# A two-layer graph kernel on one core: four more blocks transposed by DMA, eight more loaded ahead, and the x1 stores moved behind the rounds of layer 0

## What is computed

```python
h = jnp.maximum(_layernorm(x), 0.0)
# layer 0: 4-bit activations, 3-bit weights
support = jnp.matmul(act_quant(h) / act_delta, weight_q / wgt_delta) * act_delta * wgt_delta
support_q = act_quant(relu(support))
x = x + jnp.matmul(adj / s, support_q / support_delta) * s * support_delta
# layer 1, with a symmetric, normalised matrix
h = jnp.maximum(_layernorm(x), 0.0)
S = (adj + adj.T) * 0.5 + I
S = dinv[:, None] * S * dinv[None, :]      # dinv = rowsum(S) ** -0.5
x = x + (adj @ S) @ h                      # taken as adj @ (S @ h)
```

## Time and profile before

| what | value |
|---|---|
| median of 3 runs | 505.09 us (504.79 to 523.74) |
| profiled execution | 509.47 us |
| its span | 507.7 us |
| TensorE busy | 489.5 us (96%) |
| VectorE busy | 275.9 us (54%) |
| ACT busy | 142.7 us (28%) |
| GpSimd busy | 36.5 us (7%) |
| granted clock, mean | 0.997 |

### The profile page before, as it was taken

The page is one execution under the profiler, slowest core; times in us unless marked ns, Lnnn a source line. Parts: engine busy times, 40 slices in busy tenths (PEclk is TensorE's granted clock), DMA queues, the critical chain, the costliest instruction groups (busy, mean ns, idle before and its releaser), DMA issues.

```text
span 507.7 us, 6439 instructions
## 1 busy us (share of the span) xinstructions
PE 489.5 (96%) x2446; PEld 242.4 (48%) x2446; DVE 275.9 (54%) x368; ACT 142.7 (28%) x199; POOL 36.5 (7%) x51
## 2 busy tenths in 40 slices
PE   1899999997999999999999999999999999999997
PEld 1756555553564444444444444444444444444446
DVE  4964779896979878787798767450001000100000
ACT  1885852434544153444432121240000000000000
POOL 1325511132000000000000000000000000000000
PEclk9999999998999999999999999999999999999999
DMA  8970577999934043323224332018001000010001
GB/s 293 402 298 1 187 167 207 196 168 211 305 117 146 0 125 105 102 94 113 83 83 126 104 103 83 0 48 304 21 22 41 21 21 21 21 41 21 21 21 43
DMA packets 39948, 56.89 MB, mean 112 GB/s; under 512 B 22904, under 2 KB 23160, under 8 KB 39928
## 3 DMA queue, kind: packets, MB, share of 16 engines
q1 hardware_dynamic: 37040, 46.15, 30.6%
q10 hardware_dynamic: 2888, 10.49, 7.4%
HBM read 42.99 MB, written 8.39 MB: 101 GB/s over the span
## 4 chain that ended last, share of the span: by engine, by line
PE 84%; DVE 7%; DMA 4%; ACT 2%; issue 1%; SPq 1%; POOL 0%; ACTq 0%
PE ps_a L1098 31%; PE ps_p L997 14%; PE ps_p L1061 7%; PE ps_a L1061 7%; PE ps_b L1061 7%; PE ps_m L1061 4%; PE ps_h L1061 4%; DMA feat<-in_x 2%; DMA at<-at 2%; PE ps_b L979 1%; PE ps_b L951 1%; PE ps_m L997 1%; PE ps_h L997 1%; PE ps_a L979 1%; DVE at L801 1%; DVE small L849 1%
## 5 line engine op out<-in xcount | busy, mean ns | idle before, releaser
L997 PE MATMUL ps_p<-small,at 128*128 128x512 f16 x448 | 102.6, 384 | 2.8 <-DMA at<-at 2.8
L920 DVE SCALAR_TENSOR_TENSOR feat<-ps_a,feat 128x512 f32<-128x512 f32 (+1 forms) x16 | 10.8, 675 | 148.7 <-PE ps_a L1098 144.2
L1098 PE MATMUL ps_a<-small,at 128*128 128x512 f16 x360 | 80.1, 379 | 0.0
L1098 PE MATMUL ps_a<-a_in,at 128*128 128x512 f16 x360 | 80.1, 379 | 0.0
L997 PEld LDWEIGHTS ps_p<-small,at 128*128 128x128 f16 x448 | 44.1, 99 | 52.2 <-issue 5.6
L499 ACT ACTIVATE split<-a_in 128x1024 f16<-128x1024 f32 x30 | 31.7, 1057 | 101.8 <-PE ps_p L1061 90.0
L1098 PEld LDWEIGHTS ps_a<-a_in,at 128*128 (+1 forms) x360 | 35.2, 98 | 42.5
L1098 PEld LDWEIGHTS ps_a<-small,at 128*128 (+1 forms) x360 | 35.2, 98 | 42.5
L845 DVE TENSOR_TENSOR split<-a_in,split 128x1024 f16<-128x1024 f32 x30 | 36.7, 1225 | 34.0 <-ACT split L499 34.0
L1061 PE MATMUL ps_p<-feat,split 128*128 (+1 forms) x180 | 43.9, 379 | 0.5 <-DVE small L849 0.5
L1061 PE MATMUL ps_a<-feat,split 128*128 (+1 forms) x180 | 43.7, 379 | 0.0
(11 more groups left out here) (178 smaller groups left out, 445.0 us busy)
## 6 DMA issues: line engine op xcount, KB each, us to landing
a_in<-in_adj SPq DMA_DIRECT2D x34, 512.0 KB, 3.7
a_in<-in_adj ACTq DMA_DIRECT2D x20, 512.0 KB, 5.0
out<-feat SPq DMA_DIRECT2D x31, 256.0 KB, 2.5
feat<-in_x SPq DMA_DIRECT2D x8, 512.0 KB, 11.3
at<-in_adj SPq DMA_DIRECT2D x8, 512.0 KB, 14.1
feat<-out SPq DMA_DIRECT2D x4, 1024.0 KB, 9.6
at<-in_L_gnn_weight SPq DMA_DIRECT2D x2, 512.0 KB, 3.8
split<-in_adj SPq DMA_DIRECT2D x1, 512.0 KB, 15.8
```

What stands on the lines that cost most here:

```text
L920: nc.vector.scalar_tensor_tensor(out, products, 1.0 / (SA * SZ), out, ALU.mult, ALU.add).then_inc(y_out, 1)
L997: last = nc.tensor.matmul(l0_bank(r), at_block(r, lo, j), small[:, j * D:(j + 1) * D], start=(j == 0 and lo == 0), stop=(j == T - 1 and lo ...
L1098: last = nc.tensor.matmul(BANK[n], at_block(t, lo, j), z_part(j, z_lo), start=(j == 0 and lo + z_lo == 0), stop=(j == T - 1 and lo == 1))
```

## The change

- Moved are units 3, 5, ..., 29 (fourteen) instead of 7, 9, ..., 25 (ten). `ADDED` has fifteen units instead of twelve. TensorE makes four turns fewer (3, 5, 27, 29); `acc` is still turned.
- Twenty units are loaded ahead instead of twelve: units 12 to 19 go to the scratch in tiles 10 to 13, as soon as `hT`, `sq`, `xq` and the weights there are done with. A unit `u` from 12 to 27 is written to a tile in which `waited_in(u)` stood, and its writers wait for these.
- Units 3 and 5 are split and moved ahead of round 1, 7 and 9 in round 1, and `2r + 7` in round `r` from 2 to 11: one round earlier than before, measured from their use.
- SP's queue now issues all loads (`rows_again` is its own), in the order of the diff. ACT's queue issues none.
- `store_x1(0)` to `store_x1(12)` are issued one behind the other, after `sums(5)`, instead of one a round.
- GpSimd's first copy into `acc` waits for `hT_ready` instead of `sq_ready`.

The diff, cut to its core:

```diff
-AHEAD = 12
+AHEAD = 20
-MOVED = tuple(range(7, 26, 2))
-ADDED = (1, 3) + MOVED
+MOVED = tuple(range(3, 30, 2))
+ADDED = (1,) + MOVED
...
+        def in_tile(u):
+            return u // 2 + 4
+        def waited_in(u):
+            return 2 * (u // 2) - 8, 2 * (u // 2) - 7
...
-        TURNS = {r: [2 * r + 4] for r in range(2, 11)}
-        TURNS.update({1: [4, 5, 6], 11: [26, 27], 12: [28, 29, "acc"], 13: [30, 31]})
-        ROW_SUMS = {4: [0, 1], 5: [2, 3], 6: [4, 5], 8: [6, 8], "acc": []}
-        MOVES = {r: [2 * r + 5] for r in range(1, 11)}
+        TURNS = {r: [2 * r + 4] for r in range(2, 12)}
+        TURNS.update({1: [4, 6], 12: [28, "acc"], 13: [30, 31]})
+        ROW_SUMS = {2: [0, 1], 4: [2, 4], "acc": []}
+        MOVES = {r: [2 * r + 7] for r in range(2, 12)}
+        MOVES[1] = [7, 9]
...
             sums(0)
             sums(1)
+            sp.wait_ge(hT_ps, T // 2)
+            rows(16)
+            rows(17)
+            move(3)
+            sp.wait_ge(sup_ps, T // 2)
+            for u in (18, 19, 12, 13):
+                rows(u)
+            sp.wait_ge(sq_ready, T // 2)
+            rows(14)
+            rows(15)
+            move(5)
+            for u in range(AHEAD, AHEAD + 4):
+                rows_again(u)
             for r in range(1, 12):
-                for u in MOVES.get(r, []):
+                if r >= 8:
+                    rows_again(2 * r + 9)
+                for u in MOVES[r]:
                     move(u)
-                store_x1(r - 1)
+                if r >= 8:
+                    rows_again(2 * r + 8)
             for v in range(2, 6):
-                free_slot(sp, UNITS - 6 + v)
+                free_slot(UNITS - 6 + v)
                 sums(v)
-            store_x1(11)
-            store_x1(12)
+            for t in range(13):
+                store_x1(t)
...
             scale_support(5)
+            hi_rows(3)
             scale_support(6)
             scale_support(7)
             hi_turned(2)
-            hi_turned(3)
+            hi_rows(5)
+            for w in ROW_SUMS[2]:
+                row_sum(w)
...
             clamp_rows(7)
+            lo_rows(3)
             clamp_support(6)
             clamp_support(7)
             lo_turned(2)
-            lo_turned(3)
+            lo_rows(5)
...
             layer0(0, [14, 15])
-            turn(3)
             for r in range(1, 14):
```

More of the change, by code:

```diff
@@ L97, in stage @@
         def stage(u, lo):
+            if u == 29:
+                return late(15, 2048 + lo * W, W, f16)
             return late(14, 2048 * (MOVED.index(u) % 2) + lo * W, W, f16)
@@ L116, in turn_no @@
             if u == "acc":
-                return turn_no(29) + 1
-            return TURNED.index(u) + (u > 29)
+                return turn_no(28) + 1
+            return TURNED.index(u) + (u > 28)
         def turn_bank(u):
@@ L202, in gnn_kernel @@
         at4 = at[:, :].rearrange("p (r two i) -> p r two i", two=2, i=N)
+        def in_tile(u):
+            return u // 2 + 4
+        def waited_in(u):
+            return 2 * (u // 2) - 8, 2 * (u // 2) - 7
         def unit_in(u):
             if RING <= u < AHEAD:
-                return late((9, 8, 7, 6)[(u - RING) // 2], u % 2 * 2 * W, W, f32)
+                return late(in_tile(u), u % 2 * 2 * W, W, f32)
             return a_in[:, (u % RING) * W:(u % RING + 1) * W]
@@ L270, in wait_moved @@
                 engine.wait_ge(at_moved[k % 2][lo], 16 * (k // 2 + 1))
[L272 to L284, removed]
         def arrivals(u):
@@ L293, in load_x, with rows, rows_again, free_slot @@
                 sp.dma_start(feat3[:, 2 * n:2 * n + 2, :], x_tiles[:, 2 * n:2 * n + 2, :]).then_inc(x_in[n], 16)
+            def rows(u):
+                sp.dma_start(unit_in(u), adj[(u // 2) * P:(u // 2 + 1) * P, (u % 2) * W:(u % 2 + 1) * W])\
+                  .then_inc(arr_sem(u), 16)
+            def rows_again(u):
+                free_slot(before(u))
+                rows(u)
+            def free_slot(u):
+                if u in ADDED:
+                    sp.wait_ge(acc_done, ADDED.index(u) + 1)
+                if u in MOVED:
+                    sp.wait_ge(lo_ready, MOVED.index(u) + 1)
+                else:
+                    sp.wait_ge(turned, turn_no(u) + 1)
+                    sp.wait_ge(rs_done, TURNED.index(u) + 1)
             def move(u):
@@ L297, in move @@
                     sp.wait_ge(ready, MOVED.index(u) + 1)
-                    if u == 13:
-                        free_slot(sp, 10 + lo)
+                    if u == 29:
+                        wait_moved(sp, 25)
+                        wait_moved(sp, 27)
+                    elif u >= 12:
+                        free_slot(waited_in(u)[lo])
                     sp.dma_start_transpose(at_half(u // 2, lo, u % 2).rearrange("p (b i) -> p b i", i=P), stage(u, lo))\
@@ L315, in _ @@
                 load_x(n)
-            rows(sp, 0)
-            rows(sp, 1)
+            rows(0)
+            rows(1)
             for n in range(2, T // 2):
                 load_x(n)
-            for u in range(2, AHEAD):
-                rows(sp, u)
+            for u in range(2, 12):
+                rows(u)
             sums(0)
             sums(1)
+            sp.wait_ge(hT_ps, T // 2)
[4 more added lines that the diff above has]
+            for u in (18, 19, 12, 13):
+                rows(u)
+            sp.wait_ge(sq_ready, T // 2)
[4 more added lines that the diff above has]
+                rows_again(u)
             for r in range(1, 12):
-                for u in MOVES.get(r, []):
+                if r >= 8:
+                    rows_again(2 * r + 9)
+                for u in MOVES[r]:
                     move(u)
-                store_x1(r - 1)
+                if r >= 8:
+                    rows_again(2 * r + 8)
             for v in range(2, 6):
-                free_slot(sp, UNITS - 6 + v)
+                free_slot(UNITS - 6 + v)
                 sums(v)
-            store_x1(11)
-            store_x1(12)
+            for t in range(13):
+                store_x1(t)
             for v in range(6, UNITS):
@@ L400, in _ @@
                 if k == 0:
-                    pool.wait_ge(sq_ready, T // 2)
+                    pool.wait_ge(hT_ready, T // 2)
                     nc.gpsimd.tensor_scalar(acc, unit_in(u), 0.0, 1.0, ALU.add, ALU.mult).then_inc(acc_done, 1)
@@ L428, in row_sum @@
                 nc.scalar.activation(unit_in(u), unit_in(u), ACT.Copy, accum_out=rowsum[:, u:u + 1]).then_inc(rs_done, 1)
-            def rows_again(u):
-                free_slot(act, before(u))
-                rows(act, u)
             def hi_rows(u):
@@ L445, in hi_turned @@
                 act.wait_ge(turned, turn_no(u) + 1)
-                if u == 12:
-                    act.wait_ge(rs_done, TURNED.index(10) + 1)
+                if 12 <= u < 28:
+                    act.wait_ge(rs_done, TURNED.index(waited_in(u)[0]) + 1)
                 nc.scalar.activation(at_half(u // 2, 0, u % 2), turn_bank(u)[:, :], ACT.Copy, scale=SA)\
@@ L533, in _ @@
                     if u == 28:
-                        wait_moved(act, MOVED[-2])
-                        wait_moved(act, MOVED[-1])
+                        wait_moved(act, 25)
+                        wait_moved(act, 27)
+                    elif u == 30:
+                        wait_moved(act, 29)
                     if u != "acc":
                         hi_turned(u)
[L538 to L541, removed]
                     if u == TURNS[r][0]:
@@ L546, in _ @@
                         row_sum(w)
-                        if w < 4 or 12 <= w < UNITS - 4:
-                            rows_again(w + (AHEAD if w < 4 else RING))
                 if r == 9:
@@ L661, in lo_turned, with lo_rows @@
                 dve.wait_ge(athi, TURNED.index(u) + 1)
-                if u == 12:
-                    dve.wait_ge(acc_done, ADDED.index(11) + 1)
-                    dve.wait_ge(lo_ready, MOVED.index(11) + 1)
+                if 12 <= u < 28:
+                    dve.wait_ge(acc_done, ADDED.index(waited_in(u)[1]) + 1)
+                    dve.wait_ge(lo_ready, MOVED.index(waited_in(u)[1]) + 1)
                 nc.vector.scalar_tensor_tensor(at_half(u // 2, 1, u % 2), turn_bank(u)[:, :], SA,
                                                at_half(u // 2, 0, u % 2), ALU.mult, ALU.subtract).then_inc(atlo, 1)
+            def lo_rows(u):
+                dve.wait_ge(hi_ready, MOVED.index(u) + 1)
+                nc.vector.scalar_tensor_tensor(stage(u, 1), unit_in(u), SA, stage(u, 0), ALU.mult, ALU.subtract)\
+                  .then_inc(lo_ready, 1)
             def scales():
@@ L797, in turned_out @@
                     lo_turned(u)
[L799 to L802, removed]
             dve.wait_ge(zeroed, 1)
@@ L974, in turn @@
                     pe.wait_ge(atlo, turn_before(u))
-                if u in (2, 3):
-                    pe.wait_ge(sup_out, T // 2 - 3 + u)
+                if turn_no(u) in (2, 3):
```

(1 more changed line is left out.)

## The result

| | before | changed |
|---|---|---|
| median | 505.88 us (18 runs, 502.83 to 523.74) | 510.62 us (18 runs, 509.02 to 511.80) |
| profiled execution | 509.47 us | 510.99 us |
| its span | 507.7 us | 509.2 us |
| granted clock, mean | 0.997 | 0.993 |

The ratio is 1.0106, with a 95% interval of 1.0083 to 1.0128; it leaves out the longest runs of the kernel before (over 1.5% above its fastest), so it isn't quite the quotient of the two medians. The time is in the range and within two per cent, but it moved up where I had said 504. The runs also lie closer together: the changed kernel's spread over 2.8 us, those of the kernel before over 20.9. That turned out to be half of the answer.

What follows compares the result with a forecast made beforehand. TensorE, busy 489.5 of 507.7 us, was taken to bound the kernel. Savings of 8.2 us against 7.3 us lost at block 3 gave -0.9 us, from 505.09 to 504.2, said as 504; range 497 to 512.

Steps and rivals of the forecast that it cites:

- The mechanism: Round 1: hi_rows(9) on ACT waits for unit 5, delaying x1_tile(1) and so TensorE at block 3; cost 7.3 us.
- the stall at 117: Layer 0, block 9: the 2.80 us wait for a transposing DMA and its slow clock go, saving 4.5 us.
- the 0.26 us: TensorE's wait for VectorE at 57.05, at turn(8) in round 1, counted as gone: 0.3 us saved.
- Turns, 3.5 us: Units 3, 5, 27 and 29 are no longer turned on TensorE: 4 x 0.87 = 3.5 us saved.
- the wait ahead of block 3: TensorE waits 5.6 us for x1_tile(1) before block 3, then loses 1.7 us to a slower clock: 7.3 us.
- my 56.1: Time at which unit 5 lands on SP's queue, after six loads and two transposes; block 2 wants it at 57.4.
- my 52.5: Landing of the last of six loads ahead of unit 5 on SP's queue: 42.0 + 3.8 + 5 x 1.33.
- the rule of the Trainium skill that the prediction quotes: Transposing DMAs are as fast as plain ones, 350 to 400 GB/s; unit 5 lands 2.2 us earlier, time 502.
- 0 to 2.4 us on lo_rows(7): Round 1, VectorE: delay of lo_rows(7) by GpSimd's adds, taken at the middle, 1.2 us.
- The clamps: Early 16-bit clamps on VectorE meeting GpSimd's adds: 0 to 0.5 us cost to TensorE, taken as 0.
- Rounds 2 to 11 and the stores: VectorE and ACT back in step by round 4, transposes with slack, x1 stores landing before their readers: cost 0.
- Rival (c): Unit 5's transposes land 6.7 us later, at 62.8, stopping block 2 and delaying x1_tile(1): 512 us, chance 0.22.

Runs made afterwards that it cites:

- the two later executions: The kernel before, unchanged, profiled twice more: 504.54 us in the first and 502.80 us in the second.

## Why the prediction was wrong

The mechanism was right, and two sizes in the sum were wrong. The sum was -8.2 + 7.3 = -0.9 us. Against an execution of the kernel before without its stall, what was measured comes to -3.74 + 10.78 = +7.04 us (the terms follow). Either error alone would have turned the sign: -8.23 + 10.78 = +2.6, and -3.74 + 7.3 = +3.6.

**The term that failed first: the stall at 117, of which I wrote "So 4.5 us go".** I took 2.80 + 1.69 us from the one profiled execution and set them off against the median of the runs. Measured from the start of turn(2) to the start of the sweep, that execution took 172.39 - 42.71 = 129.68 us; the two later executions took 125.02 and 125.03 (40.67 to 165.70 in the second):

```profile
40.67 1.04 PE L979 MATMUL ps_a<-ident,a_in 128*128 128x128 f32 x8
...
165.70 1.46 PE L1061 MATMUL ps_a<-feat,split 128*128 128x512 f16 x6
```

The difference is 4.65 us, and the two that had no stall belong to executions of 504.54 and 502.80 us. My text had the warning in it: the profiled execution stood 4.4 us above the median, I wrote that "the difference applies to both kernels", and it was for the most part this stall. Outside this stretch only its start varies: turn(2) starts between 40.67 and 42.71 in all traces, and from the sweep on each takes 335.3 us. The changed kernel's profiled execution stands 0.4 us above its median. So in an execution without the stall, about half of them, the change could free only the four turns and the 0.26 us, 3.7 us, and not 8.2.

**Turns, 3.5 us: right.** 32 matmuls fewer, and the versions without a wait at block 3 show it: with a slot for unit 9 the stretch took 164.44 - 41.92 = 122.52 us, 2.51 less than 125.03 with the 1.15 us for the clamps still in it, so 3.66 us went, against 3.48 + 0.26 = 3.74.

**The term that failed second, the wait ahead of block 3: the right place, cause, order and clock, and too short.** Said: 5.6 us and 1.7 us of slow clock; measured: 6.97 and 9.39 - 7.07 = 2.32. The low half of unit 5 landed at 55.46, and this trace runs 1.22 us ahead of the other (turn(2) at 41.49 against 42.71), so 56.7 against my 56.1. In it two errors cancel: the last load landed 7.8 us after 45.75, so at 53.6 or 54.8 on my scale, against my 52.5: SP was at the issue of move(3) until 41.87, 1.1 us later than I had it on that scale, the first load took 4.6 us instead of 3.8 to land, and the other five 7.0 instead of 6.7; and the two transposes took 1.9 us behind it where I had 3.6. By the rule of the Trainium skill that the prediction quotes ("Advanced Engine Details and Errata", section "X-Bar Transpose (TRN2)") they would take an estimated 1.4 us: behind loads on their own queue the trace is nearer to the rule than to my bound, while the 5.3 to 9.8 us to landing in the kernel before are not covered by it. What was short was the lock: "0 to 2.4 us on lo_rows(7)" left out lo_rows(9). The adds stand back to back, the next one got in between the two instructions, and both waited: 5.74 - 2.3 = 3.4 us against my 1.2. So x1_tile(1) ended 2.8 us later than I had it (70.67, or 71.9 on my scale, against 69.1). The wait grew by 1.4 us only, since TensorE, held up for 1.15 us by the clamps, itself came 1.5 us later to block 3 (63.75, or 65.0, against 63.5). The Trainium skill, "SBUF — State Buffer", section "SBUF: two separate sides", states the lock as exclusive and held for a whole instruction, the loser blocked; the trace agrees for each of the two instructions (2.47 and 3.35 us instead of 1.2).

**The clamps, "0 to 0.5 us, I take 0": 1.15 us.** For the same reason: I let one clamp wait for one add; the two waited for two, 2.6 us each. My bound was for TensorE's part, and it took more than twice that.

**Rounds 2 to 11 and the stores: right,** but for 0.34 us for a load at 127. No wait for a transposing DMA; those between 89 and 131 us land after 3.1 us at the median. ACT has no wait for a store behind the rounds, and the run with the stores back in the rounds bears out the 0 for them.

The sum with what was measured: -3.74 + 1.15 + 6.97 + 2.32 + 0.34 = 7.04, so +7.0 us against an execution of the kernel before without its stall; the stretch shows 173.88 - 41.49 - 125.03 = 7.4. The medians are 4.7 us apart, since the stall is in part of the runs of the kernel before. Rival (c), on the other side, priced a landing of unit 5 that came 6.7 us late; it landed in time, and the kernel was slower with the landing nearly as forecast. That 510.6 lies inside my range is luck: the upper part of the range was there for rival (c).

**What stays open.** Why the transposes of the kernel before get stuck in some executions. Both parts of the change, each alone, keep them from it, though the medians to landing between 89 and 131 are 5.6 and 5.3 us, those of the kernel before without the stall; what they share (fewer DMAs side by side, or another timing) these runs don't tell. Whether the loads ahead were of use beyond that wasn't tried alone.

## What to carry to other kernels

When a profiled execution stands as far above the median as a stall in it is long, suspect that the stall is an accident of that execution, and read a second trace before you count on its removal. When a wait is put into an in-order queue, follow everything behind it to the engine that bounds: here one staging slot, wanted one transfer too early on ACT, held up a PSUM bank three hand-overs later, and moving two instructions, or giving the unit a slot of its own, turned a loss of 1.1% into a gain of 0.6 to 0.8%. Beside a partner that works back to back, count up to one full wait for each instruction that may have to take turns with it, not one for the group.

## What the runs showed of the hardware

- VectorE and GpSimd take turns at what they share, instruction by instruction: four VectorE instructions of 0.4 to 1.2 us took 2.5 to 3.4 us each beside back-to-back adds of 2.35 us, the two 16-bit clamps with one SBUF input among them. The adds wait too: 3.14 to 3.16 us where they met a lo_rows. Not each one waits: with unit 5 moved ahead and with a slot for unit 9, one lo_rows of the two took 1.2 us and the other 3.4. Column sums, which read PSUM, and lo_turned, which reads one input from PSUM and one from SBUF, took their 1.2 us beside the same adds.
- After a wait of TensorE of 2.03 us the granted clock stayed at 1.00 in one execution (32 products in 7.08 us), while six of ten runs of that program show a mean of 0.996 or 0.997; after 2.80 and 6.97 us it was 0.50 for a while, at a loss of 1.7 and 2.3 us. It fell after 4.04 us too, where 29 products took 8.57 us (32 take 7.07 at the full clock). The loss doesn't grow with the wait: 2.0 us after 8.27 (9.05 us for the 32).
- Behind six loads in one queue, two transposing DMAs of 256 KB landed within 1.9 us of the last load's landing; alone, each lands 3.1 us after its issue. Between 89 and 131 us they took 4.9 to 9.4 us in the two executions of the kernel before without the stall and 5.4 to 14.3 in the one with it, 3.7 to 9.5 with the stores alone taken away, and 3.0 to 6.7 with the loads on SP's queue.
